# A fourth PSUM lane for the attention scores, a three-bank ring, and a new order table

## The reference

```python
q = einsum('bsd,dhk->bshk', x, W_Q); k = ...; v = ...
scores = einsum('bqhc,bshc->bhqs', q, k) / sqrt(64)
probs = softmax(where(causal_mask, MASK_FILL, scores))
z = einsum('bhqs,bshc->bqhc', probs, v)
x = layernorm(x + einsum('bqhc,chd->bqd', z, W_out) + b_out)
x = layernorm(x + ffn(x))     # layer norm, 256 -> 1024, silu, 1024 -> 256, halved and added
```

## Time and profile before

| | |
|---|---|
| median of 3 runs | 1804.33 us (1804.23 to 1804.38) |
| the profiled execution | 1803.28 us |
| its span, first to last instruction | 1801.5 us |
| mean granted clock of TensorE | 0.987 of 2.4 GHz |
| attention stage / feed-forward stage | up to about 1486 us / the rest |
| busy share of the span | TensorE 95%, ScalarE 83%, VectorE 76%, GpSimd 75% |

### The profile page before, as it was taken

How to read it: one execution, slowest core, us unless ns; L and a number is a source line. 1 busy time by engine, 2 the same in 40 slices (tenths; PEclk the granted TensorE clock), 3 DMA queues, 4 the chain that set the end, 5 groups by cost and what they waited for, 6 DMA issues and landing times. The chain is left out here.

```text
span 1801.5 us, 53858 instructions
## 1 busy us (share of the span) xinstructions
PE 1703.7 (95%) x21836; PEld 1209.2 (67%) x21836; DVE 1374.6 (76%) x3164; ACT 1503.7 (83%) x3165; POOL 1357.2 (75%) x826
## 2 busy tenths in 40 slices
PE   4799999999999999999999999999999985899997
PEld 2466666666666666666666666666666654789886
DVE  7979797878787778888889787979787844656553
ACT  4599999999999999999999999999999981465464
POOL 3498989898989897989888989898988890332232
PEclk9899999999999999999999999999999998999999
DMA  4013121202020202121212121111111209222200
GB/s 134 13 23 98 21 52 17 57 16 57 14 60 12 56 17 57 20 78 20 57 20 57 20 54 24 50 26 49 25 49 25 49 14 340 77 74 71 94 13 24
DMA packets 113207, 91.82 MB, mean 51 GB/s; under 512 B 73152, under 2 KB 100032, under 8 KB 111808
## 3 DMA queue, kind: packets, MB, share of 16 engines
q1 hardware_dynamic: 112960, 88.38, 18.2%
HBM read 33.82 MB, written 20.97 MB: 30 GB/s over the span
## 5 line engine op out<-in xcount | busy, mean ns | idle before, releaser
L459 POOL TENSOR_TENSOR p_lo<-p_full,p_hi 128x1024 f16<-128x1024 f32 (+1 forms) x640 | 1161.1, 1841 | 215.4 <-ACT p_full L556 212.8
L555 ACT ACTIVATE p_hi<-psum 128x512 f16<-128x512 f32 (+3 forms) x1280 | 718.7, 562 | 71.5 <-PE psum L854 42.6
L556 ACT ACTIVATE p_full<-psum 128x512 f32<-128x512 f32 (+3 forms) x1280 | 724.8, 569 | 0.0
L612 DVE TENSOR_REDUCE row_max<-psum 128x1 f32<-128x512 f32 x768 | 485.8, 682 | 30.8 <-PE psum L820 27.1
L876 PE MATMUL psum<-v,p_hi 128*128 128x65 f16 x4352 | 487.5, 193 | 5.9 <-POOL p_lo L459 3.9
L878 PE MATMUL psum<-v,p_hi 128*128 128x64 f16 x4352 | 488.9, 194 | 0.0
L880 PE MATMUL psum<-v,p_lo 128*128 128x65 f16 x4352 | 486.5, 192 | 0.0
L876 PEld LDWEIGHTS psum<-v,p_hi 128*128 128x128 f16 x4352 | 407.2, 97 | 81.5 <-POOL p_lo L459 11.5
L850 PE MATMUL psum<-qa,ka 128*128 128x512 f16 (+3 forms) x1280 | 444.4, 348 | 15.8 <-ACT p_full L556 14.8
L878 PEld LDWEIGHTS psum<-v,p_hi 128*128 128x128 f16 x4352 | 403.2, 97 | 70.9 <-issue 0.8
L854 PE MATMUL psum<-qb,kb 128*128 128x512 f16 (+3 forms) x1280 | 444.1, 348 | 1.5 <-DVE qb L625 1.4
(11 more groups left out here) (127 smaller groups left out, 2669.2 us busy)
## 6 DMA issues: line engine op xcount, KB each, us to landing
zT_dram<-z_T SPq DMA_DIRECT2D x16, 1024.0 KB, 4.2
z_rest<-zT_dram SPq DMA_DIRECT2D x5, 2048.0 KB, 10.3
qb<-qa SPq DMA_DIRECT2D x128, 64.0 KB, 1.9
ka<-ka SPq DMA_DIRECT2D x128, 64.0 KB, 1.9
shared_z<-zT_dram SPq DMA_DIRECT2D x3, 2048.0 KB, 9.8
shared_z<-xT_dram SPq DMA_DIRECT2D x8, 512.0 KB, 7.1
xs<-x_dram SPq DMA_DIRECT2D x8, 512.0 KB, 10.5
out_dram<-res SPq DMA_DIRECT2D x8, 512.0 KB, 3.2
```

The lines of the kernel that those rows point to most:

```text
L459: nc.gpsimd.tensor_tensor(p_lo[:, at % NP, cols], p_full[:, at % NP, cols], p_hi[:, at % NP, cols], ALU.subtract).then_inc(probs_split, 1)
L555: nc.scalar.activation(p_hi[:, at % NP, to], lane_bank(a)[:, P * f:QB], ACT.Exp, scale=1.0 / SCORE)
L556: nc.scalar.activation(p_full[:, at % NP, to], lane_bank(a)[:, P * f:QB], ACT.Exp, scale=1.0 / SCORE).then_inc(lane_read, 1)
L612: nc.vector.reduce_max(most, bank, AX.X).then_inc(ring_read, 1)
```

## The change

`LANES` goes from 3 to 4 and `RINGS` from 4 to 3, and `PATTERN` is another string with the same letters. Which operations there are, and what each does, stays the same. `first_order` and `background` stay too. Of the table two lines stand for all.

```diff
 PATTERN = """
-cccscspcsptcs
-cpposscscccs
...
+ccsccscspps
+tcppocscsss
...
 """.split()
 MAXES = 4
 Z_BANKS = 1
-RINGS = 4
-LANES = 3
+RINGS = 3
+LANES = 4
 Z_BUFS = 3
```

More of the change, by code:

```diff
@@ L98 @@
 PATTERN = """
-cccscspcsptcs
-cpposscscccs
[L101 to L119, removed]
+ccsccscspps
+tcppocscsss
+cccppcpcpssctsoggcs
+psscpppcscs
+cppsccpsczsps
+occvpptvcpsscpsccs
+ppccscscspcs
+pocsccsppscpcptpcpzs
+csscsccps
+ccpscscppcscpcpcos
+cgpsppsstcppcs
+sccspsccs
+ppcsppssps
+pocccspspcss
+cpcpcppccsgptssgpps
+zpspspspvpppos
+gssvss
+ppccpcscspcscs
+cpcssctpcpspcs
+tppcggppsppppsoss
+z
 """.split()
```

## The result

The changed kernel took 1809.49 us (median of 20 runs, 1805.56 to 1812.28), the kernel before beside it 1804.51 (20 runs, 1800.42 to 1808.70): a ratio of 1.0027, with a 95% interval of 1.0019 to 1.0034. It is slower by about 5 us. The prediction said no change, 1804, with a chance of 0.42 and a range of its own from 1800.7 to 1807.9. The time lies outside that range and inside the one for 8 in 10, 1797 to 1812, on the side of the slower rivals.

What follows compares the result with a forecast made beforehand. TensorE was taken to bound the quiet units, VectorE unit 0 and GpSimd the end, so only waiting could move. Terms summed to -0.4 us: 1804 us, no change, own range 1800.7 to 1807.9, 8 in 10 from 1797 to 1812.

Steps and rivals of the forecast that it cites:

- copies: First chunk of each unit, waiting for group 3's copy: -1.7 us, and +1.2 for longer landings, together -0.5 us.
- the ring in every unit: Fourth block of each unit, three banks: 0.5 us of waits off and 0.5 on in 15 units, net 0.
- (b): Passes over `wo` in units 8 and 9, two short of ring banks: +0.7 us; longer passes over x: -0.2.
- the clock: Unit 5, clock 0.98 after a 1.96 us wait: half of up to 1.9 us comes back, -0.9 us.
- `wo`: Units 10 to 13: a 0.3 us wait behind the output-weight part is covered by one more lane, -1.2 us.
- the tail: End of the attention stage, bound by GpSimd: its last `p_lo` ends earlier, -0.3 us, between -2 and +2.
- (a): Units 2 and 9: peaks step takes a ring place, so group 2 waits 1.5 us for group 1's bank, twice: +3.0.
- (c): Prologue, dense in ring steps and bound by VectorE: three banks cost +2.0 us, from 0.5 to 4.
- Rival 1: The ring's thin margins turn into waits: 0.6 us a unit makes 9 us, 1813; chance 0.33 shared with rival 3.
- rival 3: The prologue loses the bank's full wait, +4 us instead of +2: 1808; chance 0.33 shared with Rival 1.
- Side work against lanes: Scores in units 1 to 6 behind ScalarE's weight and x parts: shorter lane waits, -3.0 us.
- rival 2: The extra lane takes all score waits: 1792 with four fifths gone, 1797 with half; chance 0.25, whole or half.

## Why the prediction was wrong

The sum said -0.4 us, and the stage grew by 4.9: it is off by 5.3. The terms that came out slower than predicted are off by 11.2 us together: copies 3.4, the ring in every unit 3.0, (b) 1.6, the clock with all else 1.1, `wo` 1.0, the tail 0.8, (a) 0.3. Term (c) alone took 5.9 back, by waits that the prediction did not know of, so it is luck that the time came within 5 us of the forecast. Step by step, by the ledger:

- **"The ring in every unit ... 0"** failed, and with the copies it is what made the kernel slower. Off were 7.2 us, nearly the 15 x 0.5 it said. On were not 15 x 0.5 but 10.2, that is 0.68 a unit. The wait of 0.49 at the fourth block stood where it was said, in each of 15 units, and is gone with four ring banks; 0.07 to 0.08 each at a chunk and a product near it and 0.03 at the next chunk came on top, some 0.18 a unit, and over 15 units that is most of the 3 us. The sum had put such places at nothing, although it knew of seven with under 0.2 us to spare. Rival 1 had these thin margins and put the point of decision at 0.25 us a unit: it measured 0.20, and with the passes over 0.25. But its reads did not take longer: L612 took 668 to 694 ns in the quiet units of after too. The distances alone did it.
- **"Copies ... -0.5"** failed by 3.4 us. It looked at the first chunk of a unit alone, where the new order, walked through, came out level and measured 1.1 worse. It missed that groups 4 and 5 had moved together, so that four copies stand in a row: 1.8 us at block 2 of units 3 and 11.
- **(b)** was right in place for `wo` (0.54 us twice, 1.1 against 0.7), and failed for x: the waits around its passes grew from 3.0 to 4.0 us, where one was to grow and one to shrink.
- **"(c) The prologue ... +2.0"** failed the other way, by 5.9 us, and hid about half of the rest. Its ring part was too small, if anything: where the first 30 us of TensorE's work are done, before had lost 24.8 us and after 29.3, near the 4 us of rival 3. What it did not know is up to 5.6 us of before behind four small instructions that waited for GpSimd, and the 2.5 to 2.8 us of slow matmuls at the half clock behind them; the changed kernel had neither at that place. (Falls of the clock for 3.4 us came in the first 60 us of either kernel, not the same in each execution, so the parts of this term are rough.) The four instructions were in the trace that I had, 10 to 20 us behind the window of the earlier trace rows, and I took VectorE's busy time there for work.
- **Side work against lanes, -3.0**, was right: -3.0 measured. The longest single wait was 1.16 us and not 1.6, but with 0.20 and 0.24 at the next two scores the place costs 1.60, as worked out. The **clock** term, -0.9, described one execution: the fall in unit 5 came in one of two profiles of before. The fall that came in both, near 78 us, it left out. The **`wo`** term, -1.2, failed: the backlog moved one score on, and its wait went from 0.30 to 0.25.
- **(a)** was right: 1.5 us twice, at 303.87 and 938.16 us.

```profile
302.30 0.22 PE L856 MATMUL psum<-mask_k,ident_b 128*128 128x128 bf16 x1
303.87 0.38 PE L791 MATMUL psum<-x_hi,w_hi 128*128 128x512 f16 x1 [1.34 <-DVE qa L638]
```

These rows of TensorE in order of time in the changed kernel show how such a wait reads: the starts lie 1.57 us apart, of which 0.06 is the matmul, and the profile books 1.34, since it lets the one before run on to its modelled end.

Of rival 2 little held for this change: the waits at scores fell by 3.2 of some 17 us, since the new order packs the scores closer, as the prediction said against it. The sentence of the Trainium skill (Perfetto Trace Analysis, Identifying Performance Opportunities) that a repeated gap on the engine to be saturated can mean too little PSUM fitted the kernel before: the old table with a fourth lane has no gap left at 14/1 and 26/1. But as the bank came from the ring, that kernel took 45 us more, and a table with the same three lanes took these gaps nearly all away too.

## What to carry to other kernels

Where banks are moved from one pool to another and the order is remade, price the two halves apart, by every place at which the poorer pool is short, and multiply even 0.05 us by the units; where the sum is a difference of two large numbers, the forecast is no better than the small terms. Before trading a bank, try whether the waits are distances in the order: here a table with the old banks gave 15 us, the trade with its table cost 5. And read the durations of small instructions in the stage that bounds: a `tensor_scalar` of 18 x 18 that takes 2 us was not working but waiting here. Moving two steps by one slot made the kernel 2.4 us faster (0.9988), not the up to 5.6 us that TensorE had stood behind them.

## What the runs showed of the hardware that was not expected

- Small VectorE instructions on SBUF waited up to 2.1 us for GpSimd's instruction to end, and the profile books this as their duration, not as idle time. The same happened outside unit 0 (L709 took 1.94 us in unit 9 of before). In the twelve profiles, from 20 us on, every one of L695 to L722 that took over 0.3 us ended 0.02 to 0.03 us behind an instruction of GpSimd. Not all waited: those of one element a row (L708 took 0.15 us at 945.25 in before, L701 0.15 at 308.46 in after), those that read PSUM (L699, 0.15 to 0.18) and the reductions took no longer inside an instruction of GpSimd.
- The waits of a program of 54,000 instructions came again at the same places to 0.05 us from one execution to the next, once the first 62 us were past. What differed was the clock (in the first profile of before a mean of 0.57 from 30 to 34, from 50 to 54 and from 545 to 549 us, in the second 1.00 in all three; the one in unit 5 cost about 1.5 us), single landings of copies (1.9 to 3.8 us for the same 64 KB), and the feed-forward stage (314.4 to 319.2 us).
